# An attention loop on five engines: VectorE's and ScalarE's work in another order, and rank compares in one operation

## What is computed

```python
x = x + conv(group_norm(x))              # 3x3-block DCT, 192x192 product, GELU, inverse DCT
t = tokens(x)                            # 16 images x 256 tokens x 192
n = ln(t)
h = silu(ln(n) @ W_hidden.T + b)         # 768 columns: v (384) and gate (384)
z = silu(ln(n) @ W_qk.T + b_qk)          # 32 columns
q, k = z * gamma[0] + beta[0], z * gamma[1] + beta[1]
A = relu(q @ k.T / 256) ** 2             # per image
t = t + n + ((A @ v) * gate) @ W_out.T + b_out
u = ln(t)
logits = u @ Wr.T                        # 8 experts, the two highest are taken
t = t + sum over the 2 of softmax_weight * expert(u)   # 192 -> 768 GELU -> 192
```

## Time and profile before

| | us |
|---|---|
| median of 3 runs | 643.41 (642.64 to 645.22) |
| span of the profiled execution, first to last instruction | 639.0 |
| PE busy | 578.6 (91%) |
| DVE busy | 421.9 (66%) |
| ACT busy | 334.7 (52%) |
| POOL busy | 272.3 (43%) |

### The profile page before, as it was taken

How to read it: one execution, slowest core, us unless ns; L and a number is a source line. 1 busy time by engine, 2 the same in 40 slices (tenths; PEclk the granted TensorE clock), 3 DMA queues, 4 the chain that set the end, 5 groups by cost and what they waited for, 6 DMA issues and landing times.

```text
span 639.0 us, 14571 instructions
## 1 busy us (share of the span) xinstructions
PE 578.6 (91%) x3844; PEld 543.2 (85%) x3845; DVE 421.9 (66%) x1549; ACT 334.7 (52%) x722; POOL 272.3 (43%) x314
## 2 busy tenths in 40 slices
PE   3999999889989989988658999999999999999992
PEld 3899887777878877777558999999999999999992
DVE  4678888677887887888885555555555555555650
ACT  1533234555656666555256555555555555555650
POOL 3322332015645645554652444444444444444442
PEclk9899999989999999999959999999999999999998
DMA  8960000401111111111241333333333333332221
GB/s 269 409 268 0 0 2 19 149 13 56 57 37 43 68 38 37 68 43 38 69 120 32 51 50 50 50 50 50 50 51 51 51 51 50 54 39 39 39 26 19
DMA packets 31827, 42.41 MB, mean 66 GB/s; under 512 B 4597, under 2 KB 27798, under 8 KB 31671
## 3 DMA queue, kind: packets, MB, share of 16 engines
q0 software_dynamic: 13488, 13.74, 13.9%
q1 hardware_dynamic: 18196, 28.19, 13.7%
q10 hardware_dynamic: 114, 0.15, 0.1%
HBM read 24.49 MB, written 17.57 MB: 66 GB/s over the span
## 4 chain that ended last, share of the span: by engine, by line
PE 37%; DMA 6%; DVE 3%; issue 3%; POOL 1%; POOLq 0%; ACT 0%; DVEq 0%; ACTq 0%
PE ps L1268 35%; DMA out_rows<-const,y_id 6%; PE ps L1273 1%; PE ps L1272 1%; POOL y_id L675 1%; DVE we_lo L1222 0%; POOL out_rows L679 0%; POOLq L204 0%; DVE over L1087 0%; DVE n_tiles L1089 0%; DVE const L1246 0%; ACT we_hi L814 0%; DVE table_parts L1092 0%; DVE const L1252 0%; DVE table_parts L1097 0%
## 5 line engine op out<-in xcount | busy, mean ns | idle before, releaser
L823 ACT ACTIVATE hT<-ps,b_i_sb 128x256 f32<-128x256 f32 (+1 forms) x240 | 95.0, 446 | 119.9 <-PE ps L1268 119.8
L1268 PE MATMUL ps<-w_o_sb,hT 128*128 x852 | 145.3, 327 | 0.9 <-DVE const L1246 0.9
L679 POOL DMA_INDIRECT out_rows<-const,y_id x71 | 123.2, 1736 | 42.0 <-POOL y_id L675 29.4
L1268 PEld LDWEIGHTS ps<-w_o_sb,hT 128*128 128x128 f32 x852 | 137.5, 191 | 1.2 <-issue 1.2
L1268 PE MATMUL ps<-n_hi,we_hi 128*128 128x256 f32 (+1 forms) x480 | 129.8, 293 | 4.4 <-DVE n_hi L1230 2.5
L1268 PEld LDWEIGHTS ps<-n_hi,we_hi 128*128 128x128 f32 x480 | 92.5, 193 | 5.4 <-DVE we_lo L1222 4.9
L1268 PE MATMUL ps<-n_hi,we_lo 128*128 128x256 f32 (+1 forms) x480 | 96.4, 283 | 0.0
L1222 DVE TENSOR_TENSOR we_lo<-we_all,we_hi 128x768 fp32r<-128x768 f32 x80 | 73.2, 957 | 22.0 <-issue 20.7
L1268 PEld LDWEIGHTS ps<-n_hi,we_lo 128*128 128x128 f32 x480 | 74.8, 193 | 0.0
L1268 PE MATMUL ps<-nA_lo,we_hi 128*128 128x256 f32 (+1 forms) x240 | 67.8, 283 | 0.0
L1246 DVE TENSOR_TENSOR const<-ps,b_o_sb 128x384 f32<-128x384 f32 (+1 forms) x40 | 20.5, 512 | 69.7 <-PE ps L1268 37.5
(11 more groups left out here) (235 smaller groups left out, 1168.7 us busy)
## 6 DMA issues: line engine op xcount, KB each, us to landing
we_all<-in_w_i SPq DMA_DIRECT2D x8, 768.0 KB, 13.6
conv_only<-lists SPq DMA_DIRECT2D x31, 194.0 KB, 2.9
w_o_sb<-in_w_o SPq DMA_DIRECT2D x8, 576.0 KB, 17.8
out_rows<-X SPq DMA_DIRECT2D x16, 192.0 KB, 1.9
X<-in_x SPq DMA_DIRECT2D x1, 1536.0 KB, 11.3
out_rows<-const,y_id POOLq DMA_INDIRECT x71, 3.6
conv_only<-lists SPq DMA_DIRECT2D x9, 97.0 KB, 2.5
we_all<-in_w_hid SPq DMA_DIRECT2D x1, 776.0 KB, 7.1
```

The lines of the kernel that those rows point to most:

```text
L679: pool.indirect_dma_start(out=out, out_offset=bass.IndirectOffsetOnAxis(ap=y_id[:, odd, t:t + 1], axis=0), in_=y_sb[:, odd, t, :], in_offs ...
L823: last = act.activation(hT[:, odd, f, 0:n].unsqueeze(1), ps_h[:, b, c, 0:n].unsqueeze(1), ACT.Gelu, bias=b_i_sb[:, ds(e * FCHUNKS + f, 1)])
L1268: return pe.matmul(dst, lhsT, rhs, start=start, stop=stop)
```

## The change

- VectorE, `choose`: the two compares of the rank with 0 and 1 (two tensor_scalar of 128x16) become one tensor_tensor of 128x32 with a new constant `choice` (0 and 1).
- VectorE, `choose` is cut in two: what gives the logit difference is now `weigh(r)`. In a step the low parts of image i + 1 and the gated product of image i come right behind `choose(r)`; `weigh(r)`, `scale_tokens(r)` and `query_key(i + 1)` follow, then (in step 0) the scales of the last images, then `count(r)` and `place(r)`.
- ScalarE: the base sum of image i + 1 comes in step i, behind `n_hi`; then z and `normalise(i + 2)`; tanh and the list rows come last.

```diff
--- before.py
+++ after.py
@@ -76,7 +76,7 @@
            ("inv0a", P), ("inv0b", P), ("inv1b", P), ("inv1c", P), ("lower", EXPERTS * EXPERTS),
            ("list_base", EXPERTS), ("tile_rows", TOKENS // P), ("pair_rows", MAX_PAIRS), ("tile_no", 1),
            ("tile_at", 1), ("pair_at", 1),
-           ("ids", HALVES), ("pad_id", 1), ("bias_rows", KBB)]
+           ("ids", HALVES), ("pad_id", 1), ("choice", 2), ("bias_rows", KBB)]
 CONST_AT, CONST_W = {}, 0
 for _n, _w in _WIDTHS:
     CONST_AT[_n] = (CONST_W, CONST_W + _w)
@@ -127,6 +127,7 @@
     put("tile_at", np.arange(P)[:, None] * P - SPARE)
     put("ids", np.arange(P)[:, None] * ROWS_P + np.arange(HALVES)[None] - HALVES)
     put("pad_id", TOKENS + np.arange(P)[:, None])
+    put("choice", every * np.arange(2)[None])
     put("bias_rows", np.isin(np.arange(KBB), (BIAS_HI, BIAS_LO))[None].astype(np.float32))
     return c
 
@@ -754,16 +755,19 @@
 
             pipeline(act, conv_step, **CONV)
 
+            def base_of(i):
+
+                wait_alone(act, normed_done, i + 1, ld_const)
+                for t in range(HALVES):
+                    at = ds(i * HALVES + t, 1)
+                    last = act.activation(X[:, at, :], X[:, at, :], ACT.Identity, bias=r_bias[:, at],
+                                          scale=r_scale[:, at])
+                last.then_inc(sum_done, 1)
+
             def attn_step(i):
                 r = i - 1
-                if not absent(i):
-
-                    wait_alone(act, normed_done, i + 1, ld_const)
-                    for t in range(HALVES):
-                        at = ds(i * HALVES + t, 1)
-                        last = act.activation(X[:, at, :], X[:, at, :], ACT.Identity, bias=r_bias[:, at],
-                                              scale=r_scale[:, at])
-                    last.then_inc(sum_done, 1)
+                if isinstance(i, int) and i == 0:
+                    base_of(0)
                 if not absent(i):
                     act.wait_ge(v_ps, i + 1)
                     act.activation(v_sb[:, :, :], ps_v, ACT.Silu).then_inc(v_done, 1)
@@ -780,6 +784,13 @@
                     act.wait_ge(nT_ps, i + 2)
                     act.activation(nB_bias[0:KB, :], ps_nT[0:KB, 1, :], ACT.Copy).then_inc(nB_bias_done, 1)
                     act.activation(n_hi[:, :, :], ps_nT, ACT.Copy).then_inc(nT_hi_done, 1)
+                if not absent(i + 1) and not (isinstance(i, int) and i < 0):
+                    base_of(i + 1)
+                if not absent(i + 1):
+                    act.wait_ge(z_ps, i + 2)
+                    act.activation(zT[:, :], ps_z, ACT.Silu).then_inc(z_done, 1)
+                if not absent(i + 2):
+                    normalise(i + 2)
                 if not absent(r):
                     wait(act, scattered, r * (16 * 2 * HALVES))
                     act.wait_ge(diff_done, r + 1)
@@ -791,11 +802,6 @@
                         last = act.activation(row_a[:, t, DATA:ROW].unsqueeze(1), X[:, at, :], ACT.Identity,
                                               bias=u_bias[:, t:t + 1], scale=u_scale[:, t:t + 1])
                     last.then_inc(row_a_done, 1)
-                if not absent(i + 1):
-                    act.wait_ge(z_ps, i + 2)
-                    act.activation(zT[:, :], ps_z, ACT.Silu).then_inc(z_done, 1)
-                if not absent(i + 2):
-                    normalise(i + 2)
 
             pipeline(act, attn_step, **ATTN)
 
@@ -1035,14 +1041,16 @@
                 chain.link(dve.tensor_tensor(equal[:, :, :, :], equal[:, :, :, :], lower, ALU.mult))
                 chain.link(dve.tensor_tensor(above[:, :, :, :], above[:, :, :, :], equal[:, :, :, :], ALU.add))
                 chain.link(dve.tensor_reduce(rank[:, :, :], above[:, :, :, :], AX.X, ALU.add))
-                for c in range(2):
-                    last = dve.tensor_scalar(chosen[:, c, :], rank[:, :, :].rearrange("p t e -> p (t e)"),
-                                             float(c), None, ALU.is_equal)
-                chain.link(last)
+                pairs = (P, 2, HALVES * EXPERTS)
+                ranks = rank[:, :, :].rearrange("p t e -> p (t e)").unsqueeze(1).broadcast_to(pairs)
+                chain.link(dve.tensor_tensor(chosen[:, :, :], ranks, K("choice").unsqueeze(2).broadcast_to(pairs),
+                                             ALU.is_equal))
                 by_expert = chosen[:, :, :].rearrange("p c (t e) -> p e c t", e=EXPERTS)
                 with nc.allow_low_precision(reason="whole numbers up to 2"):
                     dve.tensor_reduce(in_row[:, :], by_expert, AX.XY, ALU.add).then_inc(in_row_done, 1)
                 dve.tensor_tensor(in_first[:, :], chosen[:, 0, 0:EXPERTS], chosen[:, 1, 0:EXPERTS], ALU.add)
+
+            def weigh(r):
 
                 both = logits[:, :, :].rearrange("p t e -> p (t e)").unsqueeze(1).broadcast_to(
                     (P, 2, HALVES * EXPERTS))
@@ -1177,10 +1185,6 @@
                 if not absent(r):
                     logits_of_tokens(r)
                     choose(r)
-                    scale_tokens(r)
-                if isinstance(i, int) and i == 0:
-                    first_scales(SCALED * HALVES, IMAGES * HALVES)
-                    second_scales(SCALED * HALVES, IMAGES * HALVES)
                 if not absent(i + 1) and not under_conv(i + 1):
                     low_parts(i + 1)
                 if not absent(i):
@@ -1189,14 +1193,20 @@
                         dve.wait_ge(av_ps, 2 * i + 1 + k)
                         dve.tensor_tensor(gatedT[:, lo:hi, :], ps_av[:, lo:hi, :], gateT[:, lo:hi, :],
                                           ALU.mult).then_inc(gated_done, 1)
+                if not absent(r):
+                    weigh(r)
+                    scale_tokens(r)
+                if not absent(i + 1):
+                    query_key(i + 1)
+                if isinstance(i, int) and i == 0:
+                    first_scales(SCALED * HALVES, IMAGES * HALVES)
+                    second_scales(SCALED * HALVES, IMAGES * HALVES)
                 if isinstance(i, int) and i == IMAGES - 1:
 
                     chain.link(dve.tensor_copy(list_earlier[:, :], list_at[:, :]))
                 if not absent(r):
                     count(r)
                     place(r)
-                if not absent(i + 1):
-                    query_key(i + 1)
                 if isinstance(i, int) and i == IMAGES - 1:
                     first_table()
```

## The result

The changed kernel runs in 622.8 us (median of 4 runs, 620.51 to 625.82); the kernel before, with one more run than was shown, in 644.32 us (642.64 to 645.3). The ratio is 0.9675, with a 95% interval from 0.9641 to 0.971. Ratios leave out the few executions that lie over 1.5% above the fastest of their kernel at a lower granted clock.

A forecast was written before the change was run, and what follows sets the result against it. Bound: a VectorE and GpSimd loop of 12.20 us a step. Steps 0 and 1 0, steps 2 to 14 +15.2, end -2.5 give 12.7 us: span 639.0 to 626.3, plus 4.4 to the median, 630.7 us (range 627.5 to 634).

The forecast's parts named there:

- steps 0 and 1: Start of the attention loop: moving the last images' scales shifts TensorE's wait to step 1; booked 0 us (-1 to +1.7).
- the end: From output product 14 to the first table: weights come later in the step, 14.8 instead of 12.25 us, a loss of 2.5.
- The difference from span to median: Whole run: the median of 643.41 us lay 4.4 above the profiled span; the same was added to the forecast span 626.3.
- The bound: Attention loop: a VectorE and GpSimd loop through the held compares makes the 12.20 us step; TensorE's gaps follow from it.
- The compare: VectorE, each step: new form alone does not free it; arriving 4.3 to 4.95 us after the weights, before GpSimd's power, does.
- The hold moves to `picked`: VectorE, each step: picked now waits for GpSimd's power and addition, up to 1.7 us long, ending with the addition.
- The step: Steps 2 to 14: new loop 11.06 us, TensorE alone 10.97; 11.05 a step taken, gaining 15.2 us.
- the first rival: Attention loop: picked hardly held, TensorE's work sets 10.90 us a step; 626.5 us, down to 623; chance 0.18.
- ScalarE's order "costs nothing": ScalarE in the loop: base sum and normalisation first, tanh and list rows last; cost nothing, without cover up to 0.5 us a step.
- Held more often: Attention loop: more small VectorE operations lie beside GpSimd's SBUF reads; 11.5 us a step, 636.8 us; chance 0.17.
- slower: Attention loop: compare still held, query/key now inside the loop; 12.92 us a step, 655 us; chance 0.04.
- does not do what it says: Attention loop: TensorE's gaps move to other waits (from_base, v behind list rows); 12.0 us a step, 643 us; chance 0.06.

## Why the prediction was right or wrong

**The forecast as a number.** It missed by 7.9 us (630.7 against 622.8). The span accounts for 4.5: steps 3.9, steps 0 and 1 1.3, the end 1.2, behind the table 0.7, less the 2.5 of the late start, which is no part of the change. The difference from span to median accounts for the other 3.4.

**The bound: right.** A loop over VectorE and GpSimd closed by the addition's hold on the compare. Moving the addition alone takes the step from 12.20 to 11.03.

**The compare: right.** Form worth nothing, place everything. It is 0.19 us for all 16 images, and 1.37 in the new form at the old place.

**The hold moves to `picked`: right in kind.** I said up to 1.7 us; it is 0.70 in the median and 1.26 at most (at 293.51, with the addition's end at 294.71), and for the first and the last image it is free (0.18).

**The step: the term that was mis-sized.** The step that failed is "TensorE alone would need 12.20 - 0.95 - 0.28 = 10.97 us a step", and the choice of 11.05 above it. Measured 10.73: 13 steps at 0.3 less are the 3.9 us between 143.55 and 139.67. TensorE is the bound now, the first rival: it has no gap from step 2 to 14, and the run with VectorE's order alone, where `picked` is free, takes the same 10.75 us a step. Two readings made it too long. TensorE's gaps were taken from modelled ends: the row said 0.95 us idle, yet without the gap the row counts and z start 0.03 us apart (207.44 and 207.47 now) instead of 1.12 (213.69 and 214.81), so the gap was worth 1.09. From z to the output product it is 0.67 now (207.47 to 208.14) and was 1.06, so the other was worth 0.39, not 0.28. 12.20 - 1.09 - 0.39 = 10.72. In the kernel after:

```profile
207.44 0.17 PE L1278 MATMUL ps<-in_row,ones_bf 128*128 128x8 bf16 x1
207.47 0.28 PE L1278 MATMUL ps<-n_hi,w_qk_hi 128*32 128x256 f32 x1
```

The loop was mis-sized as well, 11.06 against 10.74. By term, from the weights at 200.98 to those at 211.72 (taken in brackets): first scatter 1.06 (1.07), scatters 4.90 (4.98), power 0.71 (0.70), addition 1.00 (0.99), end of the held operation 0.06 (0.12), from there to query/key 1.07 (1.26), query/key 0.65 (0.72), list rows with the copy's part 1.29 (1.22). The largest error is the 1.26: it was read from the start of `picked`, so 0.2 us of `picked` itself stood in the sum beside the hold that now contains them. The chain shows no wait for a third engine, and it is no longer than TensorE's work. So the two are level, and a shorter loop alone would gain nothing more. (That the terms of such a chain add up to the step says nothing by itself: every chain that closes after one step does. What counts is that there is no idle time in it.)

**ScalarE's order "costs nothing": right, and beside the point.** I priced what it might lose and not what it allows. Without it the new VectorE order, with query/key ahead, gives back everything (12.2 a step). The place where I should have seen it: query/key waits for z, z stood behind tanh, and the change put query/key ahead of the list rows that close the loop.

**Steps 0 and 1: 0 booked, 1.3 gained.** The wait of attend for `from_base` came, 2.27 us (2.5 forecast):

```profile
138.80 2.83 PE L1278 MATMUL ps<-attnT,hT 128*128 128x256 f32 x12 [2.27 <-issue]
...
142.63 0.30 PE L1278 MATMUL ps<-n_hi,w_qk_hi 128*32 128x256 f32 x1 [0.64 <-DVE n_hi L907]
```

The clock did not drop again in this run. The two windows from 128 to 136 us show 1.00 now, where 128 to 132 showed 0.58 before:

```profile
128.00:132.00 4.00, 3.96 (x25) 3.54 (x24) 3.24 (x15) 1.91 (x5) 0.00 (x0) 1.00 0.01 2
132.00:136.00 4.00, 4.00 (x26) 3.35 (x26) 3.35 (x23) 2.04 (x3) 0.00 (x0) 1.00 0.00 0
```

That part is luck: in the run with the two compares back, with the same order in steps 0 and 1 and the same wait of 2.27 us, it was 0.64 from 140 to 144 us. There the stretch was 0.2 us longer (25.40 us against 25.19).

The compares of step 1 are later, since their first difference was held by the addition (1.07 us instead of 0.29):

```profile
139.01 1.07 DVE L1038 TENSOR_TENSOR above<-logits 128x128 f32<-128x128 f32 x1
```

**The end: 2.5 booked, 1.34 lost.** Same place and sign. The weights of the last but one image come 13.5 us behind out 14, less than the 10.33 + 4.5 that I added up.

**Span to median: 3.4 us.** Each run of the kernel after takes 1.9 to 2.1 us more than its own span. So the span of 639.0 belongs to a run of about 641 us, one that lies below the median before, and the profiled run after (623.77) is one above its median. A single profiled span is not the median's.

**Of the rivals,** TensorE-bound (626.5, down to 623) is what happened, with less chance than the forecast. "Held more often" (636.8) and "slower" (655) did not happen; "does not do what it says" (643) is what the change would have been without ScalarE's part (642.74), through a wait for z and not for the causes I named.

## What to carry to other kernels

When a small VectorE operation takes five times its usual length, look at what GpSimd has running and queued, and ask what stands behind the held instruction, not how it is written: putting operations that read PSUM into the held time gave 19 us here, rewriting the held one gave none. When an operation moves ahead of another on one engine, list for whose result it waits, and let the engine that makes that result be reordered with it. And take a gap's worth from the starts on both sides of it, against the same two starts in a step without a gap.

## What the runs showed of the hardware

- A VectorE operation on SBUF operands that starts inside GpSimd's power (0.73 us, 128x2) is free if nothing of GpSimd's is ready to follow (0.25 us for the pair), and is held to the end of the addition (128x384, 1.00 us) if that follows at once (1.37 and 1.44 us in the steps shown). The Trainium skill (SBUF — State Buffer, "Who interferes with whom") has the block between the two engines; that it depended here on what is queued behind, only these runs show, and since spans on GpSimd are rough it is a reading of start times, not an explained mechanism.
- The hold met `tensor_scalar` (1.44 for the pair before), `tensor_tensor` (1.37 for the compare, 0.64 to 1.26 for `picked`, 1.07 for `above`) and `tensor_scalar` on 32 partitions (1.50 for a pair of 0.72). It never met the gated product or the low parts, with one operand in PSUM. The pair of gated products takes 1.02 us beside the power and the addition (for 13 images in the kernel after) and without them; the second low part takes 0.43 us when it lies wholly inside the addition (14 images, with GpSimd's addition moved in the kernel before) and 0.43 elsewhere.
- TensorE's pace in the first 40 us moved the start of the loop by up to 4 us between kernels with the same convolution: 12 equal matmuls at 17 us took 2.18 us in four of the 13 profiles and 4.02 to 4.15 us in the others, and the low granted clock behind them lasted 7 or 10 us. That is more than most edits here are worth. The stretches behind it repeat far better (10.75 or 10.76 us a step over steps 3 to 14, and 22.36, 22.37, 22.36 and 22.42 us up to the output product of step 1, in the four runs with split scales).
